# Rounding two weights on ScalarE instead of VectorE, moving W_in's transposes, and halving the first context load

## The chip, the cores and the metric

The kernel runs on one core of a Trainium2 chip. The metric is the device time in microseconds of one execution; lower is better. TensorE's clock has two levels here, 1.2 and 2.4 GHz; the profile shows the granted clock of a stretch as a share of 2.4 GHz.

## What is computed

One layer of cross attention by autocorrelation, and a feed-forward layer with simulated quantisation, on x of 2048 x 256 with a context of 1601 x 256:

```python
# attention: q from layernorm(x), k and v from the context (padded to 2048)
qf = jnp.fft.rfft(qt); kf = jnp.fft.rfft(kt)
c = qf.real * kf.real + 1j * -(qf.imag * kf.imag)
corr = jnp.fft.irfft(c, n=Lq)
# mean over heads and channels, the 15 largest delays, softmax, v rolled and summed
mean_value = jnp.mean(corr, axis=(1, 2))
weights, delay = jax.lax.top_k(mean_value, top_k)
x = x + agg @ Wo + bo
# feed forward on layernorm(x)
W_in_sim = quantize_w8_per(W_in, axis=0)      # round(w * 127/amax) per column
W_out_sim = quantize_w8_per(W_out, axis=1)    # the same per row
hidden = gelu(quantize_a16(y) @ W_in_sim + b_in)
out = x + quantize_a16(hidden) @ W_out_sim + b_out
```

## The kernel before

The five engines have a program each, written by hand, in which every wait stands at its place. Positions are split as 2048 = 128 x 16 and each Fourier transform is a 128-point transform by matmul (the table F), with a second step in small blocks. TensorE's results go through eight PSUM banks in one fixed order, the list `order`; unit n may start when unit n - 8 of that list has been emptied, which `take_bank` waits for by the table `emptied`. Units that matter here:

- HT: filler matmuls (`keep_clock`). CD: the transform of the context, eight banks, two for each of four loads of 448 KB (`ld_ctx`). GG and SM: products of Wk and Wq. QP: the projection, eight banks, evicted by VectorE (`projected`), which adds a term from `steps`, for which the Pool spreads the table IB. XD: the transform of the normalised x, eight banks; ScalarE evicts the even ones and VectorE the odd ones.
- GR: four banks of gram products (`gramian`); ScalarE evicts the diagonal blocks of half the partitions and VectorE those of the other half. `second_step(i)` multiplies the blocks of bank i into UU and needs both halves. In TensorE's order they stand as gramian 0, 1, step 0, gramian 2, step 1, gramian 3, step 2, step 3.
- From UU VectorE forms the mean correlation: IN, ME, TM (L676 to L693), with WVO and BVO (products for the values) between. Then come the 15 largest values (L699 to L701), the exponentials on ScalarE (L467 to L469), and the weights wn (L710 to L715). VP are the value projections (`vproj`, L941), W1 and W2 (L1046, L1050) turn the weights into a spectrum, MX and OO apply it.
- TR and IV turn the result and apply the inverse step. VectorE adds x and takes statistics, ScalarE and VectorE normalise four quarters into `yn`, TY transposes them (L1113) with fillers between, AM1 and AM2 find the largest value for the rounding of y, and ScalarE makes `yhi` (L536) for M1 (with W_in), and M2 (with W_out) follows.

A weight is rounded in eight pieces of 128 x 256. VectorE does it in two instructions a piece: times the scale plus MAGIC (1.5 * 2**23) into the buffer wtmp, and minus MAGIC into the result. W_in's pieces (L650, L651) come after the XD copies; its transposes WB follow BVO on TensorE (L1021), and ScalarE evicts them (L459) into `winq`. W_out's pieces (L661, L662) come in twos behind each of VectorE's gram copies (L669). L645 and L654 find the largest magnitudes.

`link` chains an instruction to the next one on the same engine by a semaphore.

## Time and profile before

| | us |
|---|---|
| median of 3 runs | 196.56 (196.24 to 198.36) |
| the profiled execution | 196.93 |
| its span in the profile | 195.1 |
| PE (TensorE) busy | 168.9 (87%) |
| DVE (VectorE) busy | 141.5 (72%) |
| ACT (ScalarE) busy | 105.9 (54%) |
| POOL busy | 25.3 (13%) |
| mean granted clock of TensorE | 0.948 |

In the rows, L12 is line 12 of the kernel before; PEld are TensorE's weight loads; SPq and ACTq are DMA issues. An idle time in brackets stands just before a row's first instruction, with what ended it.

### The profile page before, as it was taken

How to read it: one execution, taken by the hardware profiler on the slowest of the kernel's cores; microseconds unless marked ns; L12 is line 12 of the kernel's file. 1: busy time of each engine (PE TensorE's matmuls, PEld its weight loads, DVE VectorE, ACT ScalarE, POOL GpSimd, SP SyncE). 2: the span in 40 equal slices, each digit the busy share in tenths (PEclk: the TensorE clock that was granted, in tenths of full speed). 3: DMA queues.
4: the chain of work that ended last, by engine and by line, in shares of the span. 5: the costliest groups of instructions: out<-in, count | busy, mean ns of one | idle time of the engine just before them, and what ended most of it. 6: DMA issues, size and time to landing. Idle time of an engine off the chain costs nothing.

```text
span 195.1 us, 2808 instructions
## 1 busy us (share of the span) xinstructions
PE 168.9 (87%) x1055; PEld 126.5 (65%) x1058; DVE 141.5 (72%) x303; ACT 105.9 (54%) x166; POOL 25.3 (13%) x30
## 2 busy tenths in 40 slices
PE   6799999982199897999979792989999997999991
PEld 4798446972199575799956382744444465888881
DVE  1006697479957767897229699579998779999974
ACT  3254339511002193142364635699989849999930
POOL 5400000200000020000000031000890001332000
PEclk9789999999559999999999998599999999999999
DMA  5999993000000000000000000000000000001215
GB/s 152 252 353 421 401 350 107 0 3 0 0 0 2 0 3 0 0 0 2 3 0 0 0 3 0 0 0 0 0 3 0 0 0 3 0 2 57 108 54 215
DMA packets 6140, 12.17 MB, mean 62 GB/s; under 512 B 560, under 2 KB 4016, under 8 KB 6000
## 3 DMA queue, kind: packets, MB, share of 16 engines
q1 hardware_dynamic: 5840, 11.85, 17.8%
q10 hardware_dynamic: 288, 0.16, 0.3%
q8 instruction: 8, 0.13, 0.3%
q14 instruction: 4, 0.03, 0.1%
HBM read 9.90 MB, written 2.10 MB: 62 GB/s over the span
## 4 chain that ended last, share of the span: by engine, by line
PE 70%; DVE 18%; ACT 5%; DMA 3%; issue 2%; DVEq 0%; SPq 0%
PE ps L1163 12%; PE ps L951 7%; PE ps L1138 7%; PE ps L1133 6%; PE ps L941 6%; PE ps L912 5%; PE ps L1073 4%; PE ps L963 4%; PE ps L974 3%; PE ps L1087 3%; DMA arena<-ctx_in_dram 3%; PE ps L1113 2%; PE ps L1062 2%; PE ps L1082 2%; DVE sm L766 2%
## 5 line engine op out<-in xcount | busy, mean ns | idle before, releaser
L1163 PE MATMUL ps<-woutq,arena 128*128 128x256 f16 x256 | 28.7, 273 | 1.3 <-ACT arena L559 0.7
L1163 PEld LDWEIGHTS ps<-woutq,arena 128*128 128x128 f16 x256 | 24.7, 98 | 5.3 <-ACT arena L559 1.5
L544 ACT ACTIVATE arena<-ps,colv,sm 128x512 f32<-128x512 f32 x32 | 23.7, 781 | 2.0 <-PE ps L1138 0.5
L866 DVE SCALAR_TENSOR_TENSOR arena<-scr,sm,arena 128x1024 f16<-128x1024 int16 x16 | 21.3, 1372 | 0.0
L845 DVE TENSOR_REDUCE sm<-arena 128x1 f32<-128x1024 f32 (+1 forms) x17 | 18.9, 1148 | 2.5 <-ACT arena L544 2.5
L1138 PE MATMUL ps<-arena,winq 128*128 128x512 bf16 x64 | 18.6, 379 | 0.1
L1133 PE MATMUL ps<-arena,winq 128*128 128x512 bf16 x61 | 17.9, 379 | 0.5 <-ACT arena L536 0.5
L559 ACT ACTIVATE arena<-arena,sm 128x1024 f16<-128x1024 f32 x15 | 16.4, 1134 | 0.0
L941 PE MATMUL ps<-wvo,arena 128*128 128x256 f32 x64 | 15.0, 385 | 0.0
L899 PE MATMUL ps<-ones 128*128 128x256 bf16 x90 | 13.8, 312 | 1.0 <-POOL ones L341 1.0
L951 PE MATMUL ps<-arena,wqk 128*128 128x512 f32 x32 | 14.0, 595 | 0.0
L607 DVE BATCH_NORM_STATS2 sm<-arena 128x6 f32<-128x256 f32 x16 | 5.5, 411 | 10.9 <-DMA arena<-x_dram 10.9
L941 PEld LDWEIGHTS ps<-wvo,arena 128*128 128x128 f32 x64 | 11.8, 190 | 2.5 <-issue 1.1
L450 ACT COPY scr<-ps 32x128 f32<-32x128 f32 x8 | 2.0, 256 | 20.1 <-PE ps L974 20.1
L899 PEld LDWEIGHTS ps<-ones 128*128 128x128 bf16 x90 | 9.8, 112 | 3.2 <-POOL ones L341 1.0
L986 PE MATMUL ps<-scr,arena 128*128 128x32 f32 x32 | 5.0, 307 | 7.8 <-DVE scr L669 7.7
L381 POOL TENSOR_TENSOR arena<-arena,rowv 128x4096 f32<-128x4096 f32 x1 | 8.9, 8876 | 19.1 <-DVE arena L820 19.1
L1138 PEld LDWEIGHTS ps<-arena,winq 128*128 128x128 bf16 x64 | 6.2, 98 | 7.7 <-DVE arena L820 0.4
L1133 PEld LDWEIGHTS ps<-arena,winq 128*128 128x128 bf16 x64 | 6.1, 98 | 7.6 <-issue 0.6
L912 PE MATMUL ps<-tabs,arena 112*128 112x128 f32 x64 | 9.0, 313 | 1.9 <-DMA arena<-ctx_in_dram 1.9
L951 PEld LDWEIGHTS ps<-arena,wqk 128*128 128x128 f32 x32 | 6.0, 190 | 7.2 <-issue 7.2
L974 PE MATMUL ps<-arena 128*128 128x128 f32 x64 | 9.9, 318 | 0.8 <-issue 0.8
(213 smaller groups left out, 301.2 us busy)
## 6 DMA issues: line engine op xcount, KB each, us to landing
tabs<-tab_dram SPq DMA_DIRECT2D x1, 2416.0 KB, 19.4
arena<-x_dram SPq DMA_DIRECT2D x4, 512.0 KB, 11.1
out_dram<-arena SPq DMA_DIRECT2D x8, 256.0 KB, 2.1
arena<-ctx_in_dram SPq DMA_DIRECT2D x4, 448.0 KB, 7.2
arena<-winT_dram SPq DMA_DIRECT2D x1, 1024.0 KB, 18.7
arena<-wout_dram SPq DMA_DIRECT2D x1, 1024.0 KB, 20.1
arena<-wqT_dram SPq DMA_DIRECT2D x1, 256.0 KB, 9.2
arena<-wkT_dram SPq DMA_DIRECT2D x1, 256.0 KB, 9.2
```

The source lines that it names most:

```text
L544: a.activation(H[:, f, 512 * c:512 * c + 512], bank("M1", n), ACT.Gelu, bias=colv[:, 6 + f:7 + f], scale=sc1[:, f:f + 1]).then_inc(S["h_re ...
L559: a.mul(piece(Hhi, n), piece(H, n), hrf[:, n % 8:n % 8 + 1]).then_inc(S["hhi_ready"], 1)
L845: ins_ = v.tensor_reduce(hm[:, n + k[0]:n + k[0] + 1], H[:, f + k[0]:f + k[0] + k[1], 512 * c:512 * c + 512], AX.XY, ALU.max, apply_absolu ...
L866: v.scalar_tensor_tensor(out=part, in0=scr16[:, n % 4, :], scalar=rf[:, f:f + 1], in1=piece(Hhi, n), op0=ALU.mult, op1=ALU.subtract).then_ ...
L899: last = t.matmul(o[:, 0:256], ones[:].bitcast(bf16)[:, 0:128], ones[:].bitcast(bf16), start=True, stop=True)
L912: last = t.matmul(o[:, 128 * k:128 * k + 128], cx[0:NC, 256 * b + 128 * h:256 * b + 128 * h + 128], F[0:NC, :], start=True, stop=True)
L941: last = t.matmul(o[:, 256 * m:256 * m + 256], ct[:, c0:c0 + 128], wvo[:, k, :], start=(k == 0), stop=(k == 1))
L951: last = t.matmul(o, wqk[:, k, 128 * h:128 * h + 128], ct[:, 2048 * k + 512 * c:2048 * k + 512 * c + 512], start=(k == 0), stop=(k == 1))
L974: last = t.matmul(o[:, 128 * m:128 * m + 128], qt[:, c0:c0 + 128], xt[:, c0:c0 + 128], start=(k == 0), stop=(k == 1))
L1133: t.matmul(o[k], winq[:, h, fs], yhi[:, h, 512 * c:512 * c + 512], start=(h == 0), stop=False)
L1138: last = t.matmul(o[k], winq[:, h, fs], ylo[:, h, 512 * c:512 * c + 512], start=False, stop=(h == 1))
L1163: return t.matmul(o[k // 2][:, 256 * (k % 2):256 * (k % 2) + 256], part[:, t0:t0 + 128], woutq[:, f, :], start=start, stop=stop)
```

## The change

- ScalarE rounds both weights, in groups of two pieces (`quantise`): two ACTIVATEs Identity with scale and bias from memory into two halves of a wider wtmp, a link, two ACTIVATEs Identity with bias negM, a link. W_in's four groups stand before and between the gram evictions and after them; two of W_out's groups stand after BVO's eviction and the other two after the exponentials.
- VectorE keeps only the scales: W_in's before its XD copies, W_out's after its first gram copy.
- The transposes WB (TensorE) and their evictions (ScalarE) move behind the inverse step, ahead of the normalised rows' transposes. This changes which unit each later bank waits for.
- The first context piece is loaded in two halves of 224 KB, and the IB table is issued on SP's queue behind wkT instead of first on ScalarE's.
- Fillers: 18 instead of 16 at the start, 14 instead of 20 behind TY 1. M2 waits for W_out's rounding.

```diff
--- before.py
+++ after.py
@@ -153,20 +153,20 @@
         scr16 = scr[:].rearrange("p n c -> p (n c)").bitcast(mybir.dt.int16)\
                       .rearrange("p (n c two) -> p n c two", n=4, two=2)[:, :, :, 0]
         winq_t = wraw[:, 0:1024].bitcast(bf16).rearrange("p (f d) -> p f d", f=8)
-        wtmp = scr[:, 3, 0:D]
+        wtmp = scr[:, 3, 0:2 * D].rearrange("p (n c) -> p n c", n=2)
         gram = scr[:, 0, 0:512].rearrange("p (g c) -> p g c", g=NG)
         pr1 = scr[:, 0, 512:1024].rearrange("p (g c) -> p g c", g=NG)
         pr2 = scr[:, 1, 0:512].rearrange("p (g c) -> p g c", g=NG)
         own = scr[0:NS, 1, 512:1024]
         ins = sb("ins", [NS, NM])
-        sm = sb("sm", [128, 704])
+        sm = sb("sm", [128, 705])
         sq = [0]
 
         def small(n, p=128):
             sq[0] += n
             return sm[0:p, sq[0] - n:sq[0]]
 
-        eps, one, posM, mhalf, ve = *(small(1) for _ in range(4)), small(4)
+        eps, one, posM, negM, mhalf, ve = *(small(1) for _ in range(5)), small(4)
         wqb = small(2)
         st = small(96).rearrange("p (b k) -> p b k", b=NB)
         mv = small(32).rearrange("p (b k) -> p b k", b=NB)
@@ -198,27 +198,28 @@
         names = ("ld_F ld_ib ld_wqk ld_tab ld_wv ld_win ld_wout ld_col ld_row "
                  "pe dve_link act_link pool_const bu_ready z_a z_d bt_zero x2b_ready nz_ready "
                  "xh_a xh_d steps_1 steps_ready dc_zero qt_ready wqk_ready wqb_ready dc_ready wvo_ready bvo_ready bvb_ready gram_a gram_d ab_ready own_ready "
-                 "mean_ready cand_ready v16_ready ex_ready eq_ready wn_ready "
+                 "ss1_ready ss2_ready wt_ready woutq_ready mean_ready cand_ready v16_ready ex_ready eq_ready wn_ready "
                  "w1_ready vh_ready mix_ready bt_ready w2_ready nm_ready os_a os_d tr_a x2_ready sd_ready "
                  "var_ready rs_ready y_a y_d yt_ready am_ready a1_ready ysc_ready winq_ready "
                  "wom_ready wg_ready rf_ready yu_ready yhi_ready yq_ready h_ready hm_ready ha_ready hsc_ready "
                  "yq_scale hhi_first hu_a hu_d hu_p nm_a nm_c hhi_ready hq_ready o_ready out_done ct_ready ones_ready rs2_ready pool_chain xt_a xt_d identb_ready").split()
         S = {n: sem(n) for n in names}
         ld_ctx = [sem(f"ld_ctx{i}") for i in range(4)]
+        ld_half = [sem(f"ld_half{i}") for i in range(2)]
         ld_xs = [sem(f"ld_x{i}") for i in range(4)]
 
 
         order = []
         order += [("HT", 0)] + [("CD", i) for i in range(8)] + [("GG", 0), ("SM", 0)]
         order += [("QP", i) for i in range(8)] + [("XD", i) for i in range(8)]
-        order += [("GR", i) for i in range(4)] + [("UU", 0), ("WVO", 0), ("IN", 0), ("BVO", 0), ("WB", 0), ("WB", 1)]
+        order += [("GR", i) for i in range(4)] + [("UU", 0), ("WVO", 0), ("IN", 0), ("BVO", 0)]
         order += [("ME", 0), ("TM", 0), ("VP", 0), ("BC", 0), ("VP", 1), ("EQ", 0), ("VP", 2), ("W1", 0), ("W2", 0)]
         order += [("VP", 3), ("VP", 4), ("VP", 5), ("MX", 0), ("MX", 1), ("VP", 6), ("VP", 7)]
         order += [("OO", i) for i in range(4)] + [("MX", 2), ("MX", 3)]
         order += [("OO", i) for i in range(4, 8)] + [("TR", 0), ("TR", 1)]
         for i in range(6):
             order += [("IV", i), ("TR", i + 2)]
-        order += [("IV", 6), ("IV", 7)]
+        order += [("IV", 6), ("IV", 7), ("WB", 0), ("WB", 1)]
         for i in range(0, 8, 2):
             order += [("TY", i), ("TY", i + 1), ("HT", 1 + i // 2)]
         order += [("AM1", 0), ("AM2", 0), ("HT", 5)]
@@ -297,10 +298,13 @@
         def _(sp):
             c3 = ctx_in.rearrange("(a b) d -> a (b d)", b=NB)
             sp.dma_start(tb("F"), tab[:, at["F"][0]:at["F"][1]]).then_inc(S["ld_F"], 16)
-            for i in range(4):
+            for h in range(2):
+                sp.dma_start(cx[0:NC, 512 * h:512 * h + 512], c3[:, 512 * h:512 * h + 512]).then_inc(ld_half[h], 16)
+            for i in range(1, 4):
                 sp.dma_start(cx[0:NC, 1024 * i:1024 * i + 1024], c3[:, 1024 * i:1024 * i + 1024]).then_inc(ld_ctx[i], 16)
             for w_s, w in ((wqT_s, wqT), (wkT_s, wkT)):
                 sp.dma_start(w_s, w.rearrange("(h p) n -> p h n", p=128)).then_inc(S["ld_wqk"], 16)
+            sp.dma_start(tb("IB"), tab[:, at["IB"][0]:at["IB"][1]]).then_inc(S["ld_ib"], 16)
             x3 = x[0].rearrange("(a b) d -> a (b d)", b=NB)
             for i in range(4):
                 sp.dma_start(xs[:, 1024 * i:1024 * i + 1024], x3[:, 1024 * i:1024 * i + 1024]).then_inc(ld_xs[i], 16)
@@ -343,6 +347,7 @@
             g.memset(one, 1.0)
             g.memset(inv[:], 1.0 / 32767.0)
             g.memset(posM, MAGIC)
+            g.memset(negM, -MAGIC)
             g.memset(eps, 1e-5)
             g.memset(mhalf, -0.5)
             g.memset(dcr[:], 0.0)
@@ -405,7 +410,6 @@
                 act.wait_ge(S["act_link"], linked[0])
 
             act.dma_start(colv[:], cols).then_inc(S["ld_col"], 16)
-            act.dma_start(tb("IB"), tab[:, at["IB"][0]:at["IB"][1]]).then_inc(S["ld_ib"], 16)
             act.wait_ge(S["pool_const"], 1)
             a.activation(warm[:, 0:1], one, ACT.Sqrt)
             for i in range(8):
@@ -443,6 +447,20 @@
             for i in range(0, 8, 2):
                 filled(act, "XD", i)
                 a.copy(spread(xt, 0, i // 2), bank("XD", i).rearrange("p (b s r) -> p b s r", b=4, r=2)).then_inc(S["xt_a"], 1)
+            win3 = wraw[:, 0:2048].rearrange("p (f d) -> p f d", f=8)
+            wou3 = wraw[:, 2048:4096].rearrange("p (f d) -> p f d", f=8)
+
+            def quantise(w3, scales, to, f):
+                for k in range(2):
+                    ins_ = a.activation(wtmp[:, k], w3[:, f + k, :], ACT.Identity, bias=posM, scale=scales[:, f + k:f + k + 1])
+                link(ins_)
+                for k in range(2):
+                    ins_ = a.activation(to[:, f + k, :], wtmp[:, k], ACT.Identity, bias=negM)
+                link(ins_)
+                return ins_
+
+            act.wait_ge(S["ss1_ready"], 1)
+            quantise(win3, ss1, winq_t, 0)
             for i in range(4):
                 filled(act, "GR", i)
                 for j in (0, 1):
@@ -450,13 +468,17 @@
                     ins_ = a.copy(gram[q, 4 * i:4 * i + 4, :],
                                   bank("GR", i).rearrange("p (g c) -> p g c", g=4)[q, :, q])
                 ins_.then_inc(S["gram_a"], 1)
+                if i < 2:
+                    quantise(win3, ss1, winq_t, 2 * i + 2)
+            quantise(win3, ss1, winq_t, 6)
+            a.copy(warm[:, 1:2], one).then_inc(S["wt_ready"], 1)
             filled(act, "WVO", 0)
             a.copy(wvo[:].rearrange("p h n -> p (h n)"), bank("WVO", 0)).then_inc(S["wvo_ready"], 1)
             filled(act, "BVO", 0)
             a.copy(bvo[:], bank("BVO", 0)[:, 0:D]).then_inc(S["bvo_ready"], 1)
-            for i in range(2):
-                filled(act, "WB", i)
-                a.copy(winq[:, i, :], bank("WB", i).bitcast(bf16)).then_inc(S["winq_ready"], 1)
+            act.wait_ge(S["ss2_ready"], 1)
+            for f in range(0, 4, 2):
+                quantise(wou3, ss2, woutq, f)
             act.wait_ge(S["bt_zero"], 1)
             for j in range(NJ):
                 q = slice(32 * j, 32 * j + 32)
@@ -467,6 +489,9 @@
             link(a.mul(negmx, v16[:, 0:1], -1.0))
             a.activation(exv[:, 0:TOPK], v16[:, 0:TOPK], ACT.Exp, bias=negmx, accum_out=zr)
             a.activation(ex, mean, ACT.Exp, bias=negmx).then_inc(S["ex_ready"], 1)
+            for f in range(4, 8, 2):
+                quantise(wou3, ss2, woutq, f)
+            a.copy(warm[:, 1:2], one).then_inc(S["woutq_ready"], 1)
 
             def mixed(*units):
                 for i in units:
@@ -519,6 +544,9 @@
             for i in range(8):
                 turned(i)
             deviation(0, 2)
+            for i in range(2):
+                filled(act, "WB", i)
+                a.copy(winq[:, i, :], bank("WB", i).bitcast(bf16)).then_inc(S["winq_ready"], 1)
             normalise(0)
             normalise(1)
             transposed(0)
@@ -634,32 +662,17 @@
             normalise_x(1)
             for i in range(4, 8):
                 projected(i)
+            dve.wait_ge(S["ld_win"], 16)
+            win3 = wraw[:, 0:2048].rearrange("p (f d) -> p f d", f=8)
+            link(v.tensor_reduce(wx, win3, AX.X, ALU.max, apply_absolute_value=True))
+            link(v.tensor_scalar(wx, wx, 1e-8, None, ALU.max))
+            link(v.reciprocal(ss1, wx))
+            v.tensor_scalar(ss1, ss1, 127.0, None, ALU.mult).then_inc(S["ss1_ready"], 1)
+
             for k in range(1, 8, 2):
                 filled(dve, "XD", k)
                 v.tensor_copy(spread(xt, 1, k // 2), bank("XD", k).rearrange("p (b s r) -> p b s r", b=4, r=2))\
                  .then_inc(S["xt_d"], 1)
-
-            dve.wait_ge(S["ld_win"], 16)
-            win3 = wraw[:, 0:2048].rearrange("p (f d) -> p f d", f=8)
-            wou3 = wraw[:, 2048:4096].rearrange("p (f d) -> p f d", f=8)
-            link(v.tensor_reduce(wx, win3, AX.X, ALU.max, apply_absolute_value=True))
-            link(v.tensor_scalar(wx, wx, 1e-8, None, ALU.max))
-            link(v.reciprocal(ss1, wx))
-            link(v.tensor_scalar(ss1, ss1, 127.0, None, ALU.mult))
-            for f in range(8):
-                link(v.tensor_scalar(wtmp, win3[:, f, :], ss1[:, f:f + 1], MAGIC, ALU.mult, ALU.add))
-                link(v.tensor_scalar(winq_t[:, f, :], wtmp, MAGIC, None, ALU.subtract))
-
-            dve.wait_ge(S["ld_wout"], 16)
-            link(v.tensor_reduce(wom, wou3, AX.X, ALU.max, apply_absolute_value=True))
-            link(v.tensor_scalar(wom, wom, 1e-8, None, ALU.max))
-            v.tensor_reduce(wg, wom, AX.X, ALU.max).then_inc(S["wom_ready"], 1)
-            link(v.reciprocal(ss2, wom))
-            link(v.tensor_scalar(ss2, ss2, 127.0, None, ALU.mult))
-
-            def quantise_out(f):
-                link(v.tensor_scalar(wtmp, wou3[:, f, :], ss2[:, f:f + 1], MAGIC, ALU.mult, ALU.add))
-                link(v.tensor_scalar(woutq[:, f, :], wtmp, MAGIC, None, ALU.subtract))
 
             dve.wait_ge(S["ld_tab"], 16)
             for i in range(4):
@@ -669,8 +682,14 @@
                     ins_ = v.tensor_copy(gram[q, 4 * i:4 * i + 4, :],
                                          bank("GR", i).rearrange("p (g c) -> p g c", g=4)[q, :, q])
                 ins_.then_inc(S["gram_d"], 1)
-                for f in range(2 * i, 2 * i + 2):
-                    quantise_out(f)
+                if i == 0:
+                    dve.wait_ge(S["ld_wout"], 16)
+                    wou3 = wraw[:, 2048:4096].rearrange("p (f d) -> p f d", f=8)
+                    link(v.tensor_reduce(wom, wou3, AX.X, ALU.max, apply_absolute_value=True))
+                    link(v.tensor_scalar(wom, wom, 1e-8, None, ALU.max))
+                    v.tensor_reduce(wg, wom, AX.X, ALU.max).then_inc(S["wom_ready"], 1)
+                    link(v.reciprocal(ss2, wom))
+                    v.tensor_scalar(ss2, ss2, 127.0, None, ALU.mult).then_inc(S["ss2_ready"], 1)
 
             filled(dve, "UU", 0)
             link(v.tensor_tensor(pr1, bank("UU", 0).rearrange("p (g c) -> p g c", g=NG), tb3("U"), ALU.mult))
@@ -900,14 +919,16 @@
                 done(last)
 
             pe.wait_ge(S["ones_ready"], 1)
-            keep_clock(0, 16)
+            keep_clock(0, 18)
             pe.wait_ge(S["ld_F"], 16)
             for i in range(8):
                 bq, h = i // 2, i % 2
-                if h == 0:
+                if h == 0 and bq:
                     pe.wait_ge(ld_ctx[bq], 16)
                 o = take_bank(pe, "CD", i)
                 for k in range(4):
+                    if i == 0 and k % 2 == 0:
+                        pe.wait_ge(ld_half[k // 2], 16)
                     b = 4 * bq + k
                     last = t.matmul(o[:, 128 * k:128 * k + 128], cx[0:NC, 256 * b + 128 * h:256 * b + 128 * h + 128],
                                     F[0:NC, :], start=True, stop=True)
@@ -1014,13 +1035,6 @@
             for k in range(2):
                 last = t.matmul(o[:, 0:D], bvb[:, k, :], wo_s[:, k, :], start=(k == 0), stop=(k == 1))
             done(last)
-            pe.wait_ge(S["identb_ready"], 1)
-            for h in range(2):
-                o = take_bank(pe, "WB", h).bitcast(bf16)
-                for f in range(8):
-                    last = t.transpose(o[:, 128 * f:128 * f + 128], winq_t[:, f, 128 * h:128 * h + 128], identb[:])
-                done(last)
-
             pe.wait_ge(S["own_ready"], 1)
             o = take_bank(pe, "ME", 0)
             for r in range(2):
@@ -1103,6 +1117,14 @@
                 turn(i + 2)
             inverse(6)
             inverse(7)
+            pe.wait_ge(S["identb_ready"], 1)
+            pe.wait_ge(S["wt_ready"], 1)
+            for h in range(2):
+                o = take_bank(pe, "WB", h).bitcast(bf16)
+                for f in range(8):
+                    last = t.transpose(o[:, 128 * f:128 * f + 128], winq_t[:, f, 128 * h:128 * h + 128], identb[:])
+                done(last)
+
             for i in range(8):
                 pe.wait_ge(S["y_a"], i // 2 + 1)
                 pe.wait_ge(S["y_d"], i // 2 + 1)
@@ -1114,7 +1136,7 @@
                                            yn[:, 256 * b + 128 * h:256 * b + 128 * h + 128], tb("I"))
                 done(last)
                 if i % 2:
-                    keep_clock(1 + i // 2, (20, 12, 6, 4)[i // 2])
+                    keep_clock(1 + i // 2, (14, 12, 6, 4)[i // 2])
             pe.wait_ge(S["am_ready"], 1)
             o = take_bank(pe, "AM1", 0)
             done(t.transpose(o[0:1, 0:128], am, tb("I")))
@@ -1158,6 +1180,8 @@
             done(t.matmul(o[:, 0:1], inv[:], a3, start=True, stop=True))
             keep_clock(7, 8)
 
+            pe.wait_ge(S["woutq_ready"], 1)
+
             def product(o, k, part, c, f, start=False, stop=False):
                 t0 = 128 * (8 * c + k)
                 return t.matmul(o[k // 2][:, 256 * (k % 2):256 * (k % 2) + 256], part[:, t0:t0 + 128], woutq[:, f, :],
```

## Rows read from the trace of the kernel before

**Rows 1.** The page, 40 equal slices: granted clock in tenths.

```profile
PEclk9789999999559999999999998599999999999999
```

**Rows 2.** The chain of waits: start, duration, what.

```profile
6.29 9.01 PE ps L912 x64
15.29 1.73 PE ps L919 x8
...
40.68 2.20 DVE sm L645
...
58.53 0.91 PE ps L986 x8
...
63.47 0.70 DVE scr L676
...
67.80 0.89 PE ps L1021 x16
...
74.79 1.83 PE ps L941 x8
...
128.13 0.73 ACT arena L536
```

**Rows 3.** DMA issues and time from issue to landing.

```profile
L301 SPq DMA_DIRECT2D arena<-ctx_in_dram x4: 419/425/428, 1.2 to 2.6; - x4
...
DMA to landing us min/median/max: 5.0/7.2/9.1
...
arena<-wkT_dram SPq DMA_DIRECT2D x1, 256.0 KB, 9.2
...
tabs<-tab_dram ACTq DMA_DIRECT2D x1, 144.0 KB, 5.2
```

**Rows 4.** Timeline of ScalarE and TensorE at the grams.

```profile
43.57 0.52 ACT L450 COPY scr<-ps 32x128 f32<-32x128 f32 x2 [3.88 <-PE ps L974]
45.36 0.52 ACT L450 COPY scr<-ps 32x128 f32<-32x128 f32 x2 [1.26 <-PE ps L974]
...
53.07 1.88 PE L986 MATMUL ps<-scr,arena 128*128 128x32 f32 x8 [7.75 <-DVE scr L669]
```

**Rows 5.** Stretches: length, PE busy, granted clock, DMA share, GB/s.

```profile
4.50:5.00 0.50, 0.00 (x0) 1.00 1.17 341
...
7.50:8.00 0.50, 0.50 (x5) 0.50 1.09 279
```

**Rows 6.** Timeline of VectorE: W_out's maximum.

```profile
49.29 2.29 DVE L654 TENSOR_REDUCE sm<-arena 128x8 f32<-128x2048 f32 x1
```

**Rows 7.** Groups of ScalarE by form: busy us, mean ns, idle before.

```profile
L559 ACT ACTIVATE arena<-arena,sm 128x1024 f16<-128x1024 f32 x15 | 16.4, 1134 | 0.0
L551 ACT ACTIVATE scr<-arena,sm 128x1024 f32<-128x1024 f32 x8 | 9.8, 1227 | 0.0
L433 ACT ACTIVATE arena<-arena,sm 128x256 f32<-128x256 f32 x12 | 6.1, 587 | 4.4 <-DVE sm L328 4.4
...
L459 ACT COPY winq<-ps 128x1024 bf16<-128x1024 bf16 x2 | 1.9, 1016 | 0.1
```

**Rows 8.** Timeline around the exponentials.

```profile
72.78 1.28 ACT L464 ACT_TABLE_LOAD   x1
75.11 0.17 DVE L710 RECIPROCAL sm<-sm 128x1 f32<-128x1 f32 x1 [0.41 <-ACT sm L469]
81.71 0.82 ACT L481 COPY arena<-scr 32x256 f32<-32x256 f32 x2 [6.71 <-DVE scr L733]
```

**Rows 9.** Timeline around the normalised rows, and one stretch.

```profile
119.11 0.30 ACT L517 ACTIVATE sm<-sm 128x4 f32<-128x4 f32 x1 [5.04 <-DVE sm L769]
...
121.72 1.10 ACT L508 ACTIVATE arena<-arena,sm 128x256 f32<-128x256 f32 x2
...
120.93 1.97 PE L1113 MATMUL ps<-tabs,arena 128*128 128x128 f32 x8 [3.77 <-ACT arena L508]
...
120.03:123.44 3.41, 2.51 (x12) 0.50 0.00 0
```

## The prediction

> **What bounds the kernel now.** I read the chain of waits first, because a busy share (TensorE 87%, VectorE 72%, ScalarE 54%) does not say which stage ends late. In [rows 2] it runs through TensorE until the spectrum of x is done near 40 us, goes over to VectorE, and comes back only at 53.07. Between these, VectorE rounds W_in (L645 to L651, ends 49.25), then measures W_out (L654 to L658, 49.29 to 52.3), and only then evicts its half of the first gram bank. That bank had been full since 43.57 and the second since 45.36: ScalarE evicted its own halves then, and sat idle 12.7 us afterwards [rows 4]. TensorE waited 7.75 us for VectorE, and the page's clock line shows 1.2 GHz for the slices after [rows 1]. VectorE then rounds two pieces of W_out behind each bank, so the product UU is read only at 63.47 [rows 2]. A second loss is in front: TensorE is idle from 4.3 (the fillers' end) to 6.29 for the first context piece, and runs the context transform at 1.2 GHz from about 7.4 to 10.8 [rows 2, 5].
>
> **The front.** The four context pieces are issued from 1.15 to 2.6 us and land 5.0 to 9.1 later, so at 6.15, then about every 1.84, the last near 11.7 [rows 3]; 448 KB per 1.84 us is the 250 GB/s or so of [rows 5]. The IB table (144 KB) landed beside them at 6.4 [rows 3]. Moved behind wkT it frees 144 KB, about 0.55 us at that rate: the pieces land near 5.6, 7.4, 9.3 and 11.1, and the first half near 4.8. TensorE keeps busy to about 4.8 (18 instead of 16 filler matmuls, 0.21 each), so its long gap goes, and with it, I take it, the stretch at 1.2 GHz. At 2.4 GHz a piece takes 1.79, less than its spacing, so the last piece decides: 11.1 + 1.8 = 12.9, where wkT (before 12.9, now about 12.4) has landed too. The Gram product of the weights started at 15.29 [rows 2]: **−2.4**. Two more issues on SP (0.45 each) come ahead of x and the weights, but those bytes queue behind the same bytes as before; I cost them at nothing. IB now lands near 13.4, the Pool spreads it in 2.1, and the first projection needs it at 17.5; if that cover were gone each late us would be one. The 32 projection matmuls (13.9 us) and the 64 of x follow without a gap, so the gain is kept up to the grams. Bounds: −0.5 (clock still low) to −2.7.
> The Trainium skill (DMA: Bandwidth & Descriptors, Bandwidth) says to batch transfers to 1 MiB or more, against splitting one. By its fit, 2.0 us plus bytes over 436 GB/s, a piece of 448 KB takes 3.05 us, and a second fixed part would put 2.0 on the front. The trace does not agree for queued loads: they land 1.84 apart.
>
> **The grams.** All that stood between the last copy of x's spectrum and the first gram copy on VectorE goes: W_in's maximum moves ahead of the spectrum copies (2.9 us; its data land at about 30, and VectorE is free at 31.3 in the shifted schedule, so it ends at 34.2 and the copies catch up before the last bank, full at 37.6). Counted from the first gram matmul at 40.8: grams 0 and 1 are full at +2.75 and +4.55 [rows 4]. Then TensorE's order is step 0 (0.91 at 2.4 GHz [rows 2]), gram 2 (1.79), step 1 (0.91), gram 3 (1.79), step 2 and step 3 (0.91 each): +11.8. What is late next? VectorE now has W_out's maximum (3.0 us [rows 6]) queued behind gram copy 0: +2.8, copies 0.65, 3.0, copies 0.65, so gram 1 is out at +7.1; step 1 needs it at +7.25. That is tight, but covered. ScalarE: one group of two pieces is two ACTIVATEs with bias and scale from memory (0.51 apart, 0.585 the last [rows 7]) and two with a bias only. L551 has both operands from memory, L559 one, and they differ by 93 ns at 1024 columns [rows 7], so the second kind is about 0.49. Group: 1.10 + 0.03 + 0.91 + 0.03 = 2.07 us; from both sides 1.75 (no cost of the operands) to 2.3 (the second kind as dear as the first). Starting at −1, ScalarE has: group 0 to +1.1; gram copies at +2.8; group 1 to +5.4; copies; group 2 to +8.0; gram 2 copies to +8.6, needed at +9.95; gram 3 copies follow the bank. A group would have to cost over 3.1 us to delay a step. So the UU product is read at +11.85 instead of 63.47 − 40.78 = +22.7: **−10.85**. With no wait in it, the clock has no reason to fall there.
> The Trainium skill (ScalarE: Activation LUTs, Rules for kernel authors) wants plain arithmetic on VectorE, not on ScalarE, and the trace agrees on the price: 0.72 us for a piece on VectorE (eight from 43.55 to 49.29) against about 1.03. Over 16 pieces that would be 5 us more. The sum does not contain it, since only what misses the idle time counts.
>
> **W_in's transposes.** 0.89 us of TensorE [rows 2] and 1.95 us of ScalarE's evictions [rows 7] leave the stage in which the correlation is reduced. The next matmul waits for VectorE until only 0.12 before the transposes end: gain 0.12 at most, and swallowed by the next term. In their new place, behind the last inverse step (TensorE ends it near 110.3), ScalarE must wait for the first bank (0.6 us more than it would have been idle anyway) and evict both before its five normalisations: these end at 115.4 instead of 113.1, the two transposed copies at 116.5. It was idle for 5.04 us until 119.11 [rows 9], waiting for VectorE's statistics, and VectorE's maximum of the first quarter starts at 114.7, after that quarter is ready (113.9). Cost nothing; without that cover 2.3.
>
> **The exponentials.** This is the new wait. After BVO's bank fills (67.80 before), ScalarE did a copy (0.42), the two evictions (1.95), four copies of U and the table load of Exp (from 72.78 [rows 8]); VectorE's reciprocal came at 75.11 [rows 8], 7.31 after BVO. Now two W_out groups (4.13) stand where the 1.95 stood: +2.2, so 9.5 after BVO. Then 1.27 to the weights wn and the matmul at L1046: 10.75 after BVO, where it was 76.62 − 67.80 = 8.82 because TensorE had a value projection to finish [rows 2]. Net **+1.9**. By the group's bounds +1.3 to +2.4. The other two W_out groups (4.1, and a 0.2 copy) follow the exponentials, where ScalarE was idle 6.71 us until 81.71 [rows 8]: nothing. W_out is used far later, at 161.
>
> **Two clock terms.** TensorE now waits some 2.3 us for the exponentials, has 0.3 of work and waits 0.8. The nearest row is the idle time of 1.94 us in front, which the low level followed, so I take a stretch of some 3.4 us at 1.2 GHz as in front, on a TensorE that is then continuously needed: **+1.5** (0 to 1.7). At 120.93 TensorE began its last transposes after 3.77 us of idling, at 1.2 GHz [rows 9], to near 127 by the page's line [rows 1]. Now the later start of that stage leaves about 1.7 us in front of them. At 2.4 GHz they are bound by ScalarE: normalisations to 122.8 [rows 9], then four copies (2.1), table load and a small activation (1.5): 126.4 instead of 128.13 [rows 2]: **−1.7** (0 to −1.9).
>
> **Sum.** −2.4 −10.85 +1.9 +1.5 −1.7 = −11.55. The profiled execution took 196.93 (span 195.1 and 1.83 around it), so 185.4. It was 0.37 over the median of 196.56; I forecast 185.2.
>
> **Rivals.**
> 1. The clock is lost behind the exponentials, and the late stage keeps its low clock: +1.7, 187.0. For: both rest on idle times between those whose outcome the trace shows.
> 2. The clock isn't lost there and is won late: −1.5, 183.7.
> 3. The front stays slow: the halves land no sooner, or the clock falls all the same. Then only about −0.6 of the −2.4 is left: 187.0. For: TensorE will still stop briefly for the second half and the second piece.
> 4. The change does not fully do what it says, because ScalarE is dearer than I work out or VectorE's W_out maximum holds gram 1. At 2.9 us per group the exponentials are 1.7 later, and at 0.5 us of a gram wait: 187.4; with the clock lost in the grams once more, 189.
> 5. Slower than before: each change between the Identity of a group and the Copy of an eviction brings a table load (1.28 [rows 8]). Place: ScalarE from the first group to W_out's last. Where it never waits it starts at 37.4 in the new schedule, and has six groups of g us and 9.5 of other work before L1046: 46.9 + 6g against 76.6, and 2g + 0.2 must fit in the 6.7 before 81.7; this turns slower at g = 4.5. Three loads a group make g = 5.9 and the kernel 208. Against: L433 and L508 are Identities between Copies without a load [rows 7, 9]. The Trainium skill (ScalarE: Activation LUTs, Table sets: the hidden batching unit) says that copy and identity are in every set; the trace agrees.
>
> **Chances.** Forecast, with both clock terms or neither (184.3 to 186.2): 0.45. Rival 1: 0.18. Rival 2: 0.15. Rival 3: 0.13. Rival 4: 0.07. Rival 5: 0.02. The range takes in rivals 1 to 3 and the lower part of 4, widened by the bounds of the group and the front: 183.2 to 188.4. About 1% is what a measurement of this kernel tells from no change. All but rival 5 lie over 1% below 196.56; some of its small forms lie within: faster 0.97, same 0.015, slower 0.015.
>
> **What the profile after would show.** L912 starts near 5 and L919 near 12.9, with granted clock 1.00 throughout; no 7.75 us wait of L986 and clock 1.00 from there to the value projections; the UU product on VectorE at about 50.3; the reciprocal of the exponentials waiting for ScalarE by some 2.4 us; ScalarE's two kinds of ACTIVATE near 585 and 490 ns. I am wrong if L919 still starts after 14.5 (front), if a gram copy of ScalarE or VectorE releases L986 (cover gone), or if the late transposes wait for ScalarE's evictions.

## The result and the profile after

The changed kernel takes 188.34 us (median of 4 executions, 187.22 to 189.04); the kernel before took 196.53 beside it. The ratio is 0.956, with an interval of 0.948 to 0.964: 4.4% faster. The forecast was 185.2 with a range of 183.2 to 188.4. The profiled execution took 189.04 (span 187.2), where the sum said 185.4. Medians here are of all executions; ratios and intervals leave out the single ones that took over 1.5% more than the fastest of their kernel.

The changed kernel's page, clock line [rows 1]:

```profile
PEclk9999999999999975999999969999999999999999
```

The long stretch at 1.2 GHz in the grams is gone. Two shorter ones are left: slices 15 and 16, and slice 24 (109.2 to 112.6 us, over transposes and fillers that end before TensorE's next wait, so it costs nothing).

Its chain of waits [rows 2] (start, duration, what):

```profile
2.10 6.89 DMA arena<-ctx_in_dram
8.99 0.04 issue
9.03 5.71 PE ps L933 x48
14.74 1.73 PE ps L940 x8
...
47.50 1.05 PE ps L1007 x8
...
52.29 0.70 DVE scr L695
...
57.03 1.00 ACT scr L455 x2
58.05 0.92 ACT woutq L458 x2
...
63.63 1.28 ACT L486
...
67.29 0.42 PE ps L1060 x4
67.73 0.69 DVE scr L618
68.43 0.04 issue
68.47 2.07 PE ps L1064 x2
70.54 7.61 PE ps L962 x24
78.15 1.78 PE ps L1076 x16
```

Where the old chain had VectorE's rounding, this one stays on TensorE through the grams. ScalarE has come into it: its rounding of W_out (L455, L458) is what the exponentials wait for. And the value projections (L962 x24) take 7.61 us where the kernel before took 5.38. The steps against the forecast, each as the difference of two starts in the two chains or timelines:

| step | forecast | measured | from |
|---|---|---|---|
| front, to the weights' Gram product | −2.4 | −0.55 | 15.29 to 14.74 |
| first gram matmul to the UU product | −10.85 | −10.63 | 22.69 to 52.29 − 40.23 = 12.06 |
| BVO full to W1's matmul | +1.9 | +1.83 | 8.82 to 67.29 − 56.64 = 10.65 |
| W1's matmul to the first MX matmul | +1.5 | +3.25 | 7.61 to 78.15 − 67.29 = 10.86 |
| last turned copy to the first yhi | −1.7 | −1.87 | 19.44 to 120.18 − 102.61 = 17.57 |
| sum | −11.55 | −7.97 | span: −7.9 |

ScalarE's two kinds of ACTIVATE (groups by form) and the two waits at the exponentials (timelines of VectorE and TensorE):

```profile
L455 ACT ACTIVATE scr<-arena,sm 128x256 f32<-128x256 f32 x16 | 8.8, 595 | 0.2
L458 ACT ACTIVATE arena<-scr,sm 128x256 bf16<-128x256 f32 x8 | 3.6, 504 | 0.1
```

```profile
65.96 0.16 DVE L729 RECIPROCAL sm<-sm 128x1 f32<-128x1 f32 x1 [2.49 <-ACT sm L491]
...
67.29 0.41 PE L1060 MATMUL ps<-sm,tabs 128*64 128x16 f32 x4 [1.89 <-DVE sm L734]
```

The two kinds take 595 and 504 ns, against 585 and 490 in the forecast; a group takes 2.04 to 2.07 us. VectorE waits 2.49 us for ScalarE where it waited 0.41 [rows 8], and TensorE 1.89 us. The granted clock in stretches (length, PE busy, granted clock):

```profile
67.50:68.00 0.50, 0.19 (x4) 1.00 0.00 0
68.00:68.50 0.50, 0.03 (x1) 0.70 0.00 0
68.50:69.00 0.50, 0.50 (x1) 0.50 0.00 0
...
74.00:75.00 1.00, 1.00 (x4) 0.50 0.00 0
75.00:76.00 1.00, 1.00 (x6) 0.98 0.00 0
```

It falls to the 1.2 GHz level near 68.2, behind the wait, and rises only near 75.0. That is 6.8 us, twice the stretch of 3.4 us that the forecast took over from the front.

### The profile page after: what moved, and what is told of

It reads as the page before. It is cut to its first block, busy times and chain, and to the rows that moved or that the text cites. A ratio compares the mean times of both kernels' runs of the same rounds, so it can differ in the third digit from the quotient of the medians.

```text
span 187.2 us, 2806 instructions
## 1 busy us (share of the span) xinstructions
PE 168.6 (90%) x1054; PEld 123.8 (66%) x1054; DVE 131.1 (70%) x271; ACT 122.2 (65%) x200; POOL 25.3 (14%) x31
## 4 chain that ended last, share of the span: by engine, by line
PE 69%; ACT 12%; DVE 10%; DMA 4%; issue 3%; SPq 1%; DVEq 0%
PE ps L1187 13%; PE ps L972 7%; PE ps L1155 7%; PE ps L1160 7%; PE ps L962 6%; PE ps L995 4%; PE ps L1087 4%; PE ps L984 4%; DMA arena<-ctx_in_dram 4%; PE ps L933 3%; PE ps L1101 3%; PE ps L1007 2%; PE ps L1076 2%; PE ps L1096 2%; DVE sm L785 2%
## 5 line engine op out<-in xcount | busy, mean ns | idle before, releaser
L1155 PE MATMUL ps<-arena,winq 128*128 128x512 bf16 x64 | 18.5, 379 | 0.3 <-ACT arena L564 0.3
L1160 PE MATMUL ps<-arena,winq 128*128 128x512 bf16 x64 | 18.6, 379 | 0.0
L962 PE MATMUL ps<-wvo,arena 128*128 128x256 f32 x64 | 17.2, 426 | 0.0
L962 PEld LDWEIGHTS ps<-wvo,arena 128*128 128x128 f32 x64 | 13.4, 215 | 3.9 <-issue 1.8
L579 ACT ACTIVATE scr<-arena,sm 128x1024 f32<-128x1024 f32 x8 | 9.8, 1230 | 0.0
L417 ACT COPY arena<-ps 128x512 f32<-128x512 f32 x8 | 4.8, 606 | 7.1 <-PE ps L933 7.1
L933 PEld LDWEIGHTS ps<-tabs,arena 112*128 112x128 f32 x64 | 8.3, 208 | 1.8 <-DMA arena<-ctx_in_dram 1.7
## 6 DMA issues: line engine op xcount, KB each, us to landing
arena<-x_dram SPq DMA_DIRECT2D x4, 512.0 KB, 10.4
arena<-winT_dram SPq DMA_DIRECT2D x1, 1024.0 KB, 17.6
```

The source lines that it names most:

```text
L579: a.activation(scr[:, n % 4, :], piece(H, n), ACT.Identity, bias=posM, scale=hsc).then_inc(S["hu_a"], 1)
L933: last = t.matmul(o[:, 128 * k:128 * k + 128], cx[0:NC, 256 * b + 128 * h:256 * b + 128 * h + 128], F[0:NC, :], start=True, stop=True)
L962: last = t.matmul(o[:, 256 * m:256 * m + 256], ct[:, c0:c0 + 128], wvo[:, k, :], start=(k == 0), stop=(k == 1))
L1155: t.matmul(o[k], winq[:, h, fs], yhi[:, h, 512 * c:512 * c + 512], start=(h == 0), stop=False)
L1160: last = t.matmul(o[k], winq[:, h, fs], ylo[:, h, 512 * c:512 * c + 512], start=False, stop=(h == 1))
```

## The experiments

The experiments ran on other chips, where the kernel before took 197.4, 196.8 and 196.4 us, so ratios to it stand beside the medians. The profile of e7 is of an execution that took 186.28, over 3 us above its median; its times are used within a stage, and where they show how far executions of one kernel differ.

**e1: the first context piece whole.** From the changed kernel:

```diff
-            for h in range(2):
-                sp.dma_start(cx[0:NC, 512 * h:512 * h + 512], ...).then_inc(ld_half[h], 16)
-            for i in range(1, 4):
+            for i in range(4):
```

> The changed kernel, with the first context piece in one load again (the IB table stays behind wkT on SP's queue). In the changed kernel the second piece landed only at 9.0 us and TensorE waited 1.1 us for it. Theory A (the halves, with rows of 2 KB instead of 4 KB, slow what is queued behind them): the second piece lands 0.5 to 1 us earlier, L940-equivalent (weights' Gram product) starts at 14.2 or sooner if the clock holds. Rival B (the loads behind are bound by the slowest of the sixteen engines' shares, whatever the first piece's form): the second piece still lands near 9.0, TensorE starts at 5.6 to 6.1 instead of 4.8 and the Gram product starts at 14.7 to 15.3. Median by A 187.8, by B 188.5 (changed kernel 188.34).

Measured: 187.62 (186.20 to 189.14), ratio 0.951. TensorE began at 6.08 instead of 4.79, and yet the Gram product started at 13.46 instead of 14.74:

```profile
6.08 7.38 PE ps L929 x64
13.46 1.73 PE ps L936 x8
```

Theory A by this trace. The ratio (0.939 to 0.963) is not told from the changed kernel's, and the later profiles show that one execution cannot tell here, see below.

**e2: the IB table on ScalarE's queue.** The changed kernel with the load of IB moved from SP's queue back to ScalarE's, behind colv.

> The changed kernel, with the IB table issued first on ScalarE's queue again (halves kept). Theory A (its 144 KB compete with the context): halves and pieces land 0.5 us later, Gram product of the weights at 15.2, median 188.8. Rival B (it costs the context nothing, since the context's loads are held by something else, and on SP's queue it only delays the issues behind it): Gram product at 14.7 or sooner, median 188.3 or less.

Measured: 186.82 (184.62 to 188.17), ratio 0.946; Gram product at 14.00. B by the numbers, but the interval (0.935 to 0.957) contains the changed kernel's ratio, so no difference is shown.

**e3: fillers in the wait for the exponentials.**

```diff
             vproj(2)
+            keep_clock(8, 16)
             pe.wait_ge(S["wn_ready"], 1)
```

> The changed kernel, with 16 filler matmuls (1.7 us at 2.4 GHz) behind the third value projection, where TensorE waits 1.89 us for the exponentials. Theory A (the low clock from 68.2 to 75.0 us follows from that wait and costs 3.25 us between W1's matmul and the first MX matmul): the clock stays at 1.00, W1 to MX takes 7.6 instead of 10.86 us, median 185.1. Rival B (the stretch is slow for another reason, as another bank or order): 188.3, as the changed kernel.

Measured: 185.40 (185.24 to 186.37), ratio 0.943 (0.936 to 0.951; the changed kernel's starts at 0.948). The mean granted clock of the four executions is 0.989 to 0.991, where it was 0.973 to 0.981. TensorE's chain behind the wait:

```profile
67.83 1.12 PE ps L1065 x2
68.95 5.38 PE ps L962 x24
74.33 1.78 PE ps L1077 x16
```

W1's matmul started at 66.65, so it is 7.7 us to MX instead of 10.86, at a granted clock of 1.00. W1's matmul still had to wait for the exponentials. The fillers compute nothing that is used, so the clock alone was worth 3.2 us between these two matmuls: A.

**e4: W_out's rounding behind the exponentials.** From the changed kernel:

```diff
-            act.wait_ge(S["ss2_ready"], 1)
-            for f in range(0, 4, 2):
-                quantise(wou3, ss2, woutq, f)
...
             a.activation(ex, mean, ACT.Exp, bias=negmx).then_inc(S["ex_ready"], 1)
-            for f in range(4, 8, 2):
+            act.wait_ge(S["ss2_ready"], 1)
+            for f in range(0, 4, 2):
                 quantise(wou3, ss2, woutq, f)
...
             place(0)
+            quantise(wou3, ss2, woutq, 4)
             mixed(0, 1)
             place(1)
+            quantise(wou3, ss2, woutq, 6)
```

> The changed kernel, with none of W_out's rounding ahead of the exponentials: two groups behind them, one behind the first placing, one behind the second. Theory A (the two groups of 2.05 us ahead of them are what VectorE's reciprocal and TensorE waited for, and the low clock follows from that wait): the wait of 2.5 us at the reciprocal falls under 0.5, W1's matmul comes 1.8 sooner, clock 1.00 after it, in all -5: 183.3. Rival B (the wait only moves: the late groups make ScalarE's placing or evictions late): W1 1.8 sooner but ScalarE's first or second placing or MX eviction becomes the releaser on the chain, 185 to 187.

Measured: 183.16 (182.25 to 185.91), ratio 0.929. The chain has no ScalarE at the exponentials, and W1 to MX takes 7.6 us. ScalarE's timeline shows the group behind the first placing fit in front of the MX evictions:

```profile
70.86 0.91 ACT L458 ACTIVATE woutq<-scr,sm 128x256 f16<-128x256 f32 x2
72.34 0.59 ACT L496 COPY arena<-ps 128x512 f32<-128x512 f32 x1 [0.57 <-PE ps L1076]
```

It was idle for 0.57 us before the eviction, so the group delayed nothing. A: the wait that the change added cost 1.8 and brought the 3.2 of clock with it; taken out together they give −5.2 in the medians (ratio 0.921 to 0.938, against 0.948 to 0.964). This profiled execution also had the fast front that was forecast, with no wait inside the context transform:

```profile
0.98 4.02 PE ps L918 x18
5.00 8.10 PE ps L933 x64
13.10 1.73 PE ps L940 x8
```

**e5: the front alone.** The kernel before with the halves, IB behind wkT and 18 fillers.

> The kernel before with the front of the change alone: first piece in halves, IB behind wkT on SP's queue, 18 fillers. With this same front the weights' Gram product has started at 14.74 us (changed kernel), 14.14 and 13.10 (two experiments), against 15.29 before. Theory A (the front is worth what the loads allow, which differs from run to run): it starts between 13 and 14.8 with the granted clock at 1.00, and the median is 0.5 to 2.2 lower than before, about 1.4 (ratio 0.993). Rival B (the front gives nothing; the runs in which it seemed to are chance): ratio 1.00.

Measured: 195.71 (12 executions, 194.44 to 216.39) against 196.82, ratio 0.997 (0.992 to 1.002): by time not told from nothing. Its profile shows both sides. The Gram product starts at 13.82, 1.47 sooner. But in the grams, where VectorE still makes TensorE wait, the clock stays low to 61.6 us, where in the kernel before it was back near 58.6:

```profile
51.60 1.89 PE ps L991 x8
53.49 3.57 PE ps L979 x16
57.06 1.55 PE ps L991 x8
58.61 3.38 PE ps L979 x16
...
64.14 0.70 DVE scr L679
```

From L991 to the UU product it took 12.5 us, where [rows 2, 4] have 10.4. So the UU product was read at 64.14, 0.67 later than before: all of the gain in front was given back, in this execution. A for the start of the Gram product. Its span is 193.9 all the same, 1.2 below the 195.1 of the kernel before, because of a late stage that e5 does not touch. TensorE waits there for the same 3.77 us as in [rows 9], but the clock stays at 1.00:

```profile
121.60 1.09 PE L1118 MATMUL ps<-tabs,arena 128*128 128x128 f32 x8 [3.77 <-ACT arena L511]
```

The eight matmuls took 1.09 us instead of 1.97, and the last turned copy to yhi took 17.57 us instead of 19.44.

**e6: the transposes back behind BVO**, from e4, with their two evictions and their place in the order of banks.

> The kernel of e4 (183.16, W_out behind the exponentials) with W_in's transposes and their evictions back behind BVO. Theory A (the change's gain around the normalised rows, from the last turned copy to the first yhi 17.6 instead of 19.4 us, comes from the moved transposes, which make TensorE start that stage later and idle less before its last transposes, so that its clock stays up): the clock falls there again as in the kernel before, +1.9, and 0 to +0.3 at the exponentials: 185.1. Rival B (it has nothing to do with the transposes): 183.2, or 182.9 with ScalarE relieved of 1.93 us there.

Measured: 185.59 (184.56 to 186.89), ratio 0.949 (0.942 to 0.956), against 0.929 (0.921 to 0.938) for e4; +2.4 in the medians. TensorE's timeline of the last transposes, with the clock at 0.50 from 109 to 113:

```profile
108.61 1.97 PE L1135 MATMUL ps<-tabs,arena 128*128 128x128 f32 x8 [4.43 <-ACT arena L536]
```

In e4 this wait was 1.52, the group took 1.09, and the last turned copy to yhi took 17.6 instead of 19.3 us. That is A: moving the transposes did not merely cost nothing, it made TensorE start that stage later and idle less in it. One trace does not show that this keeps the clock, since in e5 it stayed up behind a wait of 3.77 us with the transposes unmoved. All profiles together speak for it: the stage takes 17.57 or 17.58 us in each of the ten with the moved transposes, and with the transposes behind BVO 19.44 (before), 19.34 (e6) and 17.57 (e5).

**e7: VectorE rounds everything, in its own idle times.** ScalarE's `quantise` is gone. VectorE's part:

```diff
+            link(v.tensor_reduce(wom, wou3, AX.X, ALU.max, apply_absolute_value=True))
+            ...                      # W_out's scales, ahead of the first gram copy
             for i in range(4):
                 filled(dve, "GR", i)
                 ...
-                if i == 0: ...       # W_out's scales
+                for f in ((0, 1), (2, 3), (4, 5), (6,))[i]:
+                    quantise(win3, ss1, winq_t, f)
...
+            quantise(win3, ss1, winq_t, 7)        # before the wait for IN
...
+            quantise(wou3, ss2, woutq, 0)         # before the copies of OO
             for i in range(1, 8, 2):
                 filled(dve, "OO", i)
                 ...
+                for f in ((1,), (2,), (3, 4), (5, 6, 7))[i // 2]:
+                    quantise(wou3, ss2, woutq, f)
```

> The changed kernel, but VectorE rounds both weights and ScalarE none: W_out's maximum ahead of the first gram copy, W_in's pieces behind the gram copies (2, 2, 2, 1 and 1 behind the UU products), W_out's pieces around the copies of the OO banks. Theory A (the gain in the grams came from what stood ahead of VectorE's gram copies, so from the place and not from the engine): the UU product is read 12.1 us or less after the first gram matmul, no wait for the exponentials, clock 1.00, and a time as e4 or a little less, 182.0 to 184. Rival B (VectorE has no room for 11.5 us of rounding, and must be relieved by ScalarE): its copies of the OO banks or the statistics behind them become late, 185 to 189.

Measured: 183.04 (182.71 to 186.28), ratio 0.937. The first gram matmul at 42.47 and the UU product at 54.38 make 11.9 us (12.06 in the changed kernel). In the OO stage the first TR matmul comes 0.3 us late (an idle time of 1.14 instead of 0.83), and nothing else there does. So A: the 10.6 us of the grams came from what stood ahead of VectorE's copies. The other engine was not needed for them.

**e8 to e11: four fronts on the kernel of e7, on one chip.** e8 has the old front (whole piece, IB first on ScalarE's queue, 16 fillers), e9 a whole piece and the rest as in the change, e10 is e7 unchanged, and e11 issues pieces 2 and 4 on ScalarE's queue.

> The kernel of e7 with the front of the kernel before: first piece whole, IB first on ScalarE's queue, 16 fillers. Theory A (the front of the change is worth what its loads allow, 0.5 to 2.2 us): the weights' Gram product starts near 15.3 with a stretch at 1.2 GHz in the context transform, and the median is 1 to 1.5 above e7 on the same chip. Rival B (nothing): equal to e7 within 0.5.

> The kernel of e7 with the first context piece whole, IB behind wkT and 18 fillers. Theory A (what counts is the fillers and the IB table out of the way, not the halves; with the halves the Gram product has started at 13.1 to 17.0, with a whole piece at 13.5): within 0.5 of e7, the Gram product at 13.3 to 14.3. Rival B (the halves are needed against the clock's fall): the clock falls in the context transform, +1.

> The kernel of e7 unchanged, so that the fronts of e8, e9 and e11 stand beside it on one chip: 183.0 as there. Its profile shows the load times of one more execution with the halves: if the start of the weights' Gram product differs from the 17.0 of e7 by more than 1 us, it is the execution and not the kernel.

> The kernel of e7 with the second and fourth context pieces issued on ScalarE's queue, the halves and the third on SP's. Theory A (the pieces wait for the slowest share of one queue, so two queues bring the second piece forward): the second piece lands before 7.5 and the Gram product starts at 13.0, 0.5 below e7. Rival B (the engines behind the queues are the same, so the pieces only interleave and the second half of the first piece lands later): the Gram product at 14 or later, 183 to 184.

| | median (all) | Gram product at |
|---|---|---|
| e8, old front | 185.57 (184.37 to 186.26) | 15.56 |
| e9, whole piece | 183.76 (182.59 to 185.01) | 13.33 |
| e10, halves | 183.50 (183.13 to 184.12) | 14.82 |
| e11, two queues | 187.07 (185.99 to 187.75) | 18.46 |

No execution of e8 was as fast as the slowest of e10: on this kernel the front is worth 2.1 us, theory A and more than the 1 to 1.5 that it expected, near the −2.4 of the forecast and not the −0.55 of the first profile. The chains of e8 and e9 show where it lies:

```profile
6.40 9.16 PE ps L917 x64
```

```profile
5.90 7.42 PE ps L917 x64
```

Of the 2.2 us between the two starts of the Gram product, 1.7 is the pace of the context transform, and only 0.5 its earlier start. Two things change from e8 to e9, the place of IB and the two fillers, and no run takes them apart on this kernel. The halves are worth nothing that shows (e9, A). e10 starts the Gram product 2.2 us sooner than e7, so the 16.99 of e7 was the execution and not the kernel. Two queues are 3.6 us worse: B for the Gram product, though B's time of 183 to 184 was missed too. The halves land 5.7 and 6.9 us after their issue instead of 3.0 to 3.3 (e10), TensorE waits for both, and the clock falls to 1.2 GHz in the transform.

How far the loads differ between executions of one kernel shows in the landing times of the three pieces behind the halves, in the same code, e4 first and e7 second (SP's issues of L304):

```profile
DMA to landing us min/median/max: 5.3/6.6/7.9
```

```profile
DMA to landing us min/median/max: 7.6/9.2/10.1
```

In e10 the first of these pieces landed after 7.1 us. The starts of the Gram product with this front are 13.10 (e4), 13.60 (e6), 13.82 (e5), 14.14 (e3), 14.74 (changed kernel), 14.82 (e10) and 16.99 (e7). The clock adds to the spread. e7 and e10 are one kernel, and TensorE waited about as long for the second piece, but the 48 matmuls behind it took 7.25 us in e7 and 5.62 in e10:

```profile
9.73 7.25 PE L921 MATMUL ps<-tabs,arena 112*128 112x128 f32 x48 [2.23 <-DMA arena<-ctx_in_dram]
```

```profile
9.20 5.62 PE L921 MATMUL ps<-tabs,arena 112*128 112x128 f32 x48 [2.28 <-DMA arena<-ctx_in_dram]
```

## Why the prediction was right, and where it was off

The direction, the chain and the place of every step were right; the sum was 3.6 us too low in the profiled execution, from two terms. That the median still lies in the range is luck: it is 0.06 us under the upper end, 3.1 above the forecast, and above the 187.0 of the rival that came true, the slow front, since the loss behind the exponentials was twice its term on top of that. (By the sum the median would be 185.0; the 185.2 was set between that and the profiled execution's 185.4.) One sign of being wrong that the forecast named did come: the Gram product started after 14.5, at 14.74.

**The first clock term (+1.5) was mis-sized: 3.25.** The mechanism was right, as e3 and e4 show: the clock fell behind the wait for the exponentials. It did so in all three profiled executions that have this wait (the changed kernel, e1 and e2), and in neither that lacks it (e3, e4). But I bounded the loss at 1.7 by the one stretch of 3.4 us in front, and the low stretch lasted 6.8 us, although TensorE was busy from 68.5 on. The bound came from a single row, while the clock line [rows 1] already showed a stretch of about 10 us in the grams, and the forecast itself read one from 120 to near 127 us.

**The front (−2.4) was wrong as a sure term.** The profiled execution gave 0.55, e8 against e10 measured 2.1, and e5, on the kernel before, nothing that its times show. The landing times of 7.4, 9.3 and 11.1 that it assumed are those of e4; the profiled execution had 9.0 for the first of these pieces. I read them out of one execution and gave no spread. The rival that the front stays slow (0.13) described the profiled execution. There the clock was at 1.00, and TensorE waited 1.09 us for the second piece; the halves cost nothing that the times of e9 and e10 show. Why the landing differs so much between executions stays open. The fit that the forecast quotes is given by the Trainium skill (DMA: Bandwidth & Descriptors, Anatomy of one DMA — SWDGE (gpsimd) path) for DMAs issued by GpSimd. These loads are issued by SP, so their spacing of 1.84 us does not test it.

**The grams (−10.85)** measured −10.63. The one cover that I called tight held to within 0.05 us: gram 2 ended at 47.45 and step 1 started at 47.50, with VectorE's copies of two banks from 46.76 to 48.09. What lay ahead of VectorE's copies was the cause, as e7 shows.

**The exponentials (+1.9, measured +1.83)**, the group's 2.07 us and the last clock term (−1.7, measured −1.87) held. The forecast had about 1.7 us of idle time left in front of the last transposes; it was 0.57 in the changed kernel and 1.52 in e4. As a sure gain the term was too strong: e5 got the same 17.57 us with the transposes unmoved. What the move buys is that the low clock was never on the path there in ten profiles, where it was in two of three without it.

**The unasked question** was whether ScalarE was needed. The forecast weighed the Trainium skill's rule to keep plain arithmetic on VectorE (ScalarE: Activation LUTs, Rules for kernel authors) as a price of 5 us that idle time covers. Two of ScalarE's eight groups were not covered, and cost 5 us with the clock. e7 follows the rule with the same gain in the grams and is 5.3 us below the change in the medians (ratio 0.937 against 0.956). A piece does take less on VectorE, 0.72 against 1.03 us, but the kernel's time does not show it: e4 is as fast as e7 with all rounding on ScalarE, once its groups stand behind the exponentials.

e4 and e7 beat both kernels. Their ratios (0.921 to 0.938 and 0.931 to 0.943) overlap.

## What to carry to other kernels

When an engine is late with an eviction, look first at what stands ahead of the eviction in its program. Reordering gave here what the move to another engine gave. Work moved into another engine's idle time must be checked against each wait behind it there, and a wait of 2 us on TensorE was priced here at 5, because the clock fell behind it; fillers in the wait gave 3 of them back. Whether the clock falls behind one and the same wait can differ between executions, so a clock term needs a chance or several profiles, not one row. A load time read from one execution needs a range, not a value.

## What the runs showed of the hardware

- Behind a wait of 1.86 to 1.89 us, with little work after it, the granted clock fell in three of three profiled executions (the changed kernel, e1, e2). In the changed kernel it then stayed at 1.2 GHz for 6.8 us, with TensorE busy by the records for all but the first 0.3 us.
- The same wait need not have the same outcome. Behind 3.77 us the clock was at 1.2 GHz in the kernel before and at 2.4 in e5. Of two executions of one kernel, the one with a wait of 2.23 us (e7) went on at 1.2 GHz and the one with 2.28 us (e10) at 2.4.
- The same load, behind the same issues, landed between 5.3 us (e4) and 7.1 us (e10) after its issue, and after 7.6 in e7's execution.
- In the profile with the context's loads split over two issuing queues (e11) the second half of the first piece landed later, 6.9 us after its issue instead of 3.3 (e10), not sooner.
- In e8 the clock record shows 1.00 between 7 and 10 us, but two of ScalarE's evictions, each released by a bank of the context transform whose piece had landed before 6.4, start at 8.48 and 10.19, so 1.71 apart, while later ones come 0.89 apart. The records have 6 or 7 matmuls in each of these three microseconds, and 11 in the one from 11 us. So the record can miss a low stretch.
